# Seam work between the q phases and attention moved among GpSimd, VectorE and ScalarE in a gated cross-attention and LoRA-expert block

## The chip, the cores and the metric

One core of a Trainium2 chip runs the kernel. The metric is the device time of one execution in microseconds (us), as the median of three runs. The engines are TensorE (PE; its weight loads are shown as PEld), VectorE (DVE), ScalarE (ACT), GpSimd (POOL) and SyncE (SP), which here only issues the DMAs.

## What is computed

x is 8 batches of 128 rows of 512, all in float32. First a layer norm, then cross-attention with an RMS norm inside, 32 heads of 128, a position bias and a mask; then a second layer norm and a feed-forward layer with 28 LoRA experts, of which each row takes two.

```python
def attention(h, ctx, mask, bias, ln_w, w_q, w_k, w_v, w_out):      # h = layernorm(x)
    n = h * rsqrt(mean(h * h) + 1e-5) * ln_w
    q, k, v = n @ w_q.T, ctx @ w_k.T, ctx @ w_v.T                   # 32 heads of 128
    s = where(mask, q @ k.T + bias, -inf)
    return h + (where(mask, softmax(s), 0) @ v) @ w_out.T

x = x + tanh(g_xattn) * attention(layernorm(x), ctx, mask, ...)
x = x + tanh(g_ffn) * lora_experts(layernorm(x))
```

## The kernel before, in words

**Precision.** Every large product is made from float32 values that are split in two: a leading part ("hi", made by ScalarE with a copy that rounds) and a rest ("lo" = raw - hi, a subtraction on VectorE or GpSimd). TensorE makes three matmuls for each pair: hi hi, lo hi, hi lo. In the code `lead...` makes the first and `rest...` the second.

**Stages.** The 32 heads are worked off in 16 phases of two heads. The start makes k, v and q of phase 0 in the plain way (`q_or_k`, `v_one`) and normalises x in between: VectorE's `norm_x` makes the eight normalised tiles (`layer`, L781, and L792 with `xn_done`), TensorE turns them (`turn_xn`), ScalarE and VectorE split them (`lead_xt`, `rest_xt`), and ScalarE also keeps a raw copy (`raw_xt`).

Then q of the phases 1 to 15 is made at once in `q_phase(0)` to `q_phase(14)` with Strassen's scheme in Winograd's form: seven products of half size in place of eight. It needs four sums of x's quarters, T1 to T4 (`t_form` on VectorE at L820, `lead_t` on ScalarE, `rest_t` on VectorE; T4's rest is on GpSimd at L397), made once, and for each phase four sums of the weights, S1 to S4 (`s_forms` on GpSimd at L381 to L386, `lead_s` on ScalarE, `rest_s` on GpSimd at L391), and the parts of three plain weight blocks (`lead_a`, `rest_a` at L830). TensorE makes the products in the order A11 B11, S1 T1, A12 B21, A22 T4, S2 T2, S4 B22, S3 T3 (`product`, L1285). ScalarE copies three results, VectorE adds five (`post`, L852), the last of them from two tiles in SBUF, and SyncE stores q in DRAM and loads the next weights (`load_forms`, once the weights in w_raw[WQ] have been used).

The seam follows: GpSimd splits the weights of phase 1 (`rest(WK, 1)`, `rest(WV, 1)`, `rest(WO, 0)`), makes the additive mask from the uint8 mask (L414), adds it to the bias for two heads (`add_mask(0)`, L358), and splits w_raw[WQ], which by then holds weights of the last layer (L420). Then 15 iterations run in which TensorE makes scores of phase a, k and v of phase a + 1, P V of phase a and the output product. VectorE does bias, maximum and normalisation (`add_bias` L887 and L890, `normalise` L896 to L901) and turns the probabilities with 32x32 transposes (`turn_probs`, L909), which P V (`pv`, L1171) needs. The last layer (L1427 on) closes the kernel.

**What sets the order.** Each engine has one hand-written program that it works off strictly in order, with waits on semaphores; there is no planner. `wait_ge` holds an engine and all that is queued behind it. The names that matter: `xn_done` counts normalised tiles, `s_step` GpSimd's weight sums, `qs_hi` and `qs_lo` the parts of S, `qa_hi` and `qa_lo` those of A, `t_done`, `t_hi_done`, `t_lo_dve` and `t_lo_pool` the stages of T, `q_prod` the products, `q_copied` and `q_post` the results taken away, `comb_done` the combined bias, `w_lo_done` the rests of the weights.

Of the kernel before, what the change touches and what calls it, by code (L numbers as in the profile page):

```python
# [24 lines left out]
P = 128  # L25
# [33 lines left out]
def build(nc, x, ctx_t, weights, bias, mask, g_x, g_f, ln_w, out):  # L59
    ctx = ExitStack()  # L60
    with ctx:
# [6 lines left out]
        def bank(name):  # L68
# [10 lines left out]
        tf_hi, tf_lo = sb("tf_hi", [P, TF, 2, HALF], F32R), sb("tf_lo", [P, TF, 2, HALF], F32R)  # L79
# [38 lines left out]
        hgt_hi, hgt_lo = (t[0:ERH, 2, 0, :].rearrange("p (i e s) -> p i e s", i=2, e=2) for t in (tf_hi, tf_lo))  # L118
# [3 lines left out]
                 xt_raw[:, 2:4, HALF:], xt_raw[:, 2:4, 0:HALF]]  # L122

# [59 lines left out]
        t_hi_done, t_lo_dve, t_lo_pool = sem("t_hi_done"), sem("t_lo_dve"), sem("t_lo_pool")  # L183
# [150 lines left out]
        def _(pool):  # L334
# [14 lines left out]
            def add_mask(p):  # L349
                pool.wait_ge(bias_in, (p + 1) * 16)  # L350
                for j in range(HP):
                    if isinstance(p, int) and p == 0:

                        pool.wait_ge(t_lo_dve, 3)
# [38 lines left out]

            s_forms(0)
            rest_s(0, 0, 0)
            pool.wait_ge(t_hi_done, 2)
            pool.tensor_tensor(tf_lo[:, 3, :, :], t_raw[3], tf_hi[:, 3, :, :].bitcast(F32), ALU.subtract).then_inc(t_lo_pool, 1)  # L397
# [30 lines left out]

            add_mask(LAST)
# [9 lines left out]
        def _(act):  # L439
# [122 lines left out]
            def q_phase(i):  # L562
# [27 lines left out]
                if last:  # L590
                    return
# [121 lines left out]
        def _(dve):  # L713
# [128 lines left out]
            rest_a(0, 2, 1, 1)  # L842
            t_form(2, b_block(1, 1), b_block(0, 1))
# [10 lines left out]
            def q_phase(i):  # L854
# [5 lines left out]
                dve.wait_ge(t_lo_dve, 3) if isinstance(i, int) and i == 0 else dve.wait_ge(q_post, i * POSTS)  # L860
# [12 lines left out]
            dve.wait_ge(mask_in, 16)  # L873
            ordered(dve.tensor_reduce(row_any[:, :], mask_u8[:, :, :], AX.X, ALU.max))
# [229 lines left out]
        def _(pe):  # L1104
# [174 lines left out]
            T1, T2, T3, T4 = (tuple(f[:, n, :, :] for f in (tf_hi, tf_lo)) for n in range(TF))  # L1279
# [9 lines left out]
            def q_phase(i):  # L1289
# [6 lines left out]
                if first:  # L1296
                    pe.wait_ge(t_lo_dve, 1)
# [10 lines left out]
                if first:  # L1308
                    pe.wait_ge(t_lo_pool, 1)
# [5 lines left out]
                if first:  # L1315
                    pe.wait_ge(t_lo_dve, 2)
# [10 lines left out]
                if first:  # L1327
                    pe.wait_ge(t_lo_dve, 3)
# [238 lines left out]
```

## Time and profile before

| | |
|---|---|
| median of 3 runs | 888.44 us (887.14 to 889.11) |
| the profiled execution, its own time | 888.88 us |
| its span, first to last instruction | 887.1 us |
| busy: TensorE, weight loads | 867.6 us (98%), 768.2 us (87%) |
| busy: VectorE, ScalarE, GpSimd | 655.4 us (74%), 359.6 us (41%), 308.5 us (35%) |
| start, until the first product of the q phases | to 48 us |
| q phases | 48 to 195 us |
| attention, phases 0 to 15 | 195 to 829 us |

Times in the timelines are microseconds from the start of the span. A row of a timeline gives the start, the length, the engine, the line of the code, the operation with output and inputs, how many were merged, and in square brackets how long the engine stood idle before it and who ended that. Neighbouring operations of one engine overlap by some 0.1 us, since one is taken in while the other drains. An operation that had to wait for a port shows that as a longer duration, not as idle time. Matmuls are pipelined, so the distance between two starts says more than a duration.

### The profile page before, as it was taken

To read this page: it belongs to the slowest core of one execution; us is meant where nothing else is said; L and a number is where in the kernel's file an instruction comes from. 1 tells how busy PE (TensorE), PEld (TensorE's weight loads), DVE (VectorE), ACT (ScalarE), POOL (GpSimd) and SP (SyncE) were. 2 spreads that over 40 slices of the span, in tenths; PEclk is the share of its full clock that TensorE was granted. 3 is DMA by queue.
4 is the path that set the end of the run, shared out by engine and by line. 5 is a ranking of instruction groups with operands and counts; after the bars stand their busy time and mean duration, and the time that the engine had idled before them with its cause. 6 is when DMAs were issued, how large, how long until landed. Compare 5 with 4: busy or idle time off the path is not lost.

```text
span 887.1 us, 15278 instructions
## 1 busy us (share of the span) xinstructions
PE 867.6 (98%) x5128; PEld 768.2 (87%) x5128; DVE 655.4 (74%) x1295; ACT 359.6 (41%) x966; POOL 308.5 (35%) x218
## 2 busy tenths in 40 slices
PE   8989999998999999999999999999999999999998
PEld 7868888887998989898999989898989999898786
DVE  6885655659696877778696968778686969698863
ACT  5564444444253353434252443434252524444320
POOL 1476656686132332423142323323231423222200
PEclk9999999999999999999999999999999999999999
DMA  9124454454121221212121211203121202211001
GB/s 317 39 95 154 152 190 154 156 175 143 48 100 48 76 87 37 100 34 91 47 85 39 100 60 64 95 30 100 47 77 47 100 26 98 93 52 55 18 25 71
DMA packets 29074, 78.23 MB, mean 88 GB/s; under 512 B 4352, under 2 KB 6400, under 8 KB 27136
## 3 DMA queue, kind: packets, MB, share of 16 engines
q1 hardware_dynamic: 29056, 78.00, 25.6%
q8 instruction: 10, 0.16, 0.1%
q14 instruction: 8, 0.07, 0.0%
HBM read 60.16 MB, written 17.83 MB: 88 GB/s over the span
## 4 chain that ended last, share of the span: by engine, by line
PE 85%; DVE 8%; POOL 2%; issue 2%; DMA 1%; ACT 1%; SPq 0%; POOLq 0%; DVEq 0%; ACTq 0%
PE proj_ps L1112 53%; PE proj_ps L1285 13%; PE score_ps L1143 3%; PE score_ps L1171 3%; PE proj_ps L1463 2%; DVE attn L909 2%; PE pv_ps L1171 2%; PE turn_ps L1171 2%; PE proj_ps L1229 1%; PE pv_ps L1143 1%; PE turn_ps L1143 1%; PE proj_ps L1481 1%; DMA w_raw<-in_weights 1%; PE pv_ps L1112 1%; PE turn_ps L1112 1%
## 5 line engine op out<-in xcount | busy, mean ns | idle before, releaser
L347 POOL TENSOR_TENSOR w_lo<-w_raw,w_hi 128x1024 fp32r<-128x1024 f32 x49 | 118.4, 2417 | 360.9 <-ACT w_hi L444 287.0
L909 DVE STREAM_TRANSPOSE attn<-attn 32x256 f32<-32x256 f32 x480 | 209.1, 436 | 6.7
L1112 PE MATMUL proj_ps<-w_hi,ct_hi 128*128 128x256 f32 x512 | 146.2, 285 | 0.0
L1112 PE MATMUL proj_ps<-w_lo,ct_hi 128*128 128x256 f32 x512 | 144.8, 283 | 0.0
L1112 PE MATMUL proj_ps<-w_hi,ct_lo 128*128 128x256 f32 x512 | 144.8, 283 | 0.0
L925 DVE TENSOR_TENSOR acc<-proj_ps,acc 128x512 f32<-128x512 f32 x112 | 77.5, 692 | 66.7 <-PE proj_ps L1112 65.8
L464 ACT ACTIVATE attn<-attn,neg_max 128x128 f32<-128x128 f32 x256 | 99.2, 389 | 36.4 <-DVE neg_max L890 36.4
L444 ACT ACTIVATE w_hi<-w_raw 128x1024 fp32r<-128x1024 f32 x49 | 51.9, 1058 | 122.7 <-PE proj_ps L1112 118.8
L1112 PEld LDWEIGHTS proj_ps<-w_hi,ct_lo 128*128 128x128 f32 x512 | 98.2, 192 | 0.7
L1112 PEld LDWEIGHTS proj_ps<-w_hi,ct_hi 128*128 128x128 f32 x512 | 98.2, 192 | 0.7
L1112 PEld LDWEIGHTS proj_ps<-w_lo,ct_hi 128*128 128x128 f32 x512 | 98.1, 192 | 0.0
L358 POOL TENSOR_TENSOR comb<-mask_add,bias_sb 128x1024 f32<-128x1024 f32 x32 | 76.1, 2400 | 60.4 <-DVE attn L887 60.3
L1112 PE MATMUL proj_ps<-w_hi,tf_hi 128*128 128x512 f32 x240 | 95.2, 397 | 0.0
L1112 PE MATMUL proj_ps<-ct_hi,w_hi 128*128 128x512 f32 x240 | 94.7, 394 | 0.0
L1112 PE MATMUL proj_ps<-w_lo,tf_hi 128*128 128x512 f32 x240 | 93.7, 390 | 0.0
L1112 PE MATMUL proj_ps<-ct_hi,w_lo 128*128 128x512 f32 x240 | 93.5, 389 | 0.0
L1112 PE MATMUL proj_ps<-ct_lo,w_hi 128*128 128x512 f32 x240 | 93.4, 389 | 0.0
L1112 PE MATMUL proj_ps<-w_hi,tf_lo 128*128 128x512 f32 x240 | 93.4, 389 | 0.0
L830 DVE TENSOR_TENSOR w_lo<-w_raw,w_hi 128x256 fp32r<-128x256 f32 x45 | 36.1, 803 | 30.6 <-ACT w_hi L530 30.3
L449 ACT ACTIVATE kt<-proj_ps 128x512 f32<-128x512 f32 x64 | 37.4, 588 | 50.6 <-PE proj_ps L1112 46.6
L391 POOL TENSOR_TENSOR w_lo<-w_raw,w_hi 128x256 fp32r<-128x256 f32 x60 | 46.5, 779 | 25.3 <-ACT w_hi L535 24.9
L921 DVE TENSOR_TENSOR tf_lo<-score_ps,tf_hi 128x512 fp32r<-128x512 f32 x28 | 19.4, 692 | 46.9 <-ACT tf_hi L470 46.9
(199 smaller groups left out, 1777.6 us busy)
## 6 DMA issues: line engine op xcount, KB each, us to landing
w_raw<-in_weights SPq DMA_DIRECT2D x67, 512.0 KB, 3.3
q_spill<-attn SPq DMA_DIRECT2D x60, 256.0 KB, 3.0
qt<-q_spill SPq DMA_DIRECT2D x15, 1024.0 KB, 7.3
acc<-in_x SPq DMA_DIRECT2D x4, 512.0 KB, 8.9
bias_sb<-in_bias SPq DMA_DIRECT2D x16, 128.0 KB, 2.0
out<-attn SPq DMA_DIRECT2D x8, 256.0 KB, 2.0
w_raw<-in_x SPq DMA_DIRECT2D x6, 256.0 KB, 2.9
qt<-in_ctx_t SPq DMA_DIRECT2D x4, 256.0 KB, 5.4
```

The costliest lines, as they stand in the source:

```text
L347: pool.tensor_tensor(lo, w_raw[:, k, :], hi.bitcast(F32), ALU.subtract).then_inc(w_lo_done[k], 1)
L358: pool.tensor_tensor(comb[:, j, :, :], mask_add[:, :, :], bias_sb[:, j:j + 1, :].to_broadcast([P, B, S]), ALU.add).then_inc(comb_done, 1)
L391: pool.tensor_tensor(columns(w_lo, WO, n), columns(w_raw, WO, n), columns(w_hi, WO, n).bitcast(F32), ALU.subtract).then_inc(qs_lo, 1)
L444: act.activation(w_hi[:, k, :] if hi is None else hi, w_raw[:, k, :], ACT.Copy).then_inc(w_hi_done[k], 1)
L449: act.activation(dst, proj_ps[i][:, :], ACT.Copy).then_inc(proj_copied, 1)
L464: e = act.activation(probs[:, u, i, :], probs[:, u, i, :], ACT.Exp, bias=neg_max[:, u, i:i + 1], accum_out=row_sum[:, u, i:i + 1])
L909: tr = dve.transpose(probs_t[k:k + Q32, t, :, :, q:q + Q32].rearrange("k j b q -> k (j b) q"), probs[q:q + Q32, HP * t:HP * t + HP, :, k:k ...
L925: dve.tensor_tensor(acc[:, b, :], proj_ps[b % BANKS][:, :], acc[:, b, :], ALU.add).then_inc(acc_done, 1)
L1112: mm = pe.matmul(o, lhs(l, n), rhs(r, n), start=(start and n == 0 and m == 0), stop=(stop and n == terms - 1 and m == 2))
L1143: mm = pe.matmul(score_bank(a, u)[:, i * S:(i + 1) * S], qt[:, j, b * S:(b + 1) * S], kt[:, j, b * S:(b + 1) * S], start=True, stop=True)
L1171: mm = pe.matmul(pv_bank(a, u)[:, i * S:(i + 1) * S], v_sb[:, b, j * DH:(j + 1) * DH], probs_t[:, t, j, i, :], start=True, stop=True)
L1285: mm = pe.matmul(o[:, :], w[l][:, c, :], x[r][:, c, :], start=(start and c == 0 and m == 0), stop=(c == 1 and m == 2), skip_group_check=no ...
```

## The change

- T3 and T4, and their rests, no longer have room of their own. They lie in the parts of w_hi and w_lo that belong to WV and WK (`t_form_at`), so the buffers tf_hi and tf_lo are half as large. Hence ScalarE takes the leading parts of phase 1's K weights after product 4 of the last q phase, and those of V after product 7. Before, K's came ahead of that q phase.
- GpSimd waits for `xn_done` 8 before the first weight sums.
- T4's rest is made by VectorE, between the rests for A22 and the sum T3. One semaphore, `t_lo_done`, counts all four.
- The additive mask is made by VectorE after q phase 0, beside the reduction of the mask that was there.
- At the seam GpSimd makes the two combined biases first, then the rests of K, V and the output weights. The rest of w_raw[WQ] comes after the loop over the phases, ahead of `add_mask(LAST)`.

```diff
-        tf_hi, tf_lo = sb("tf_hi", [P, TF, 2, HALF], F32R), sb("tf_lo", [P, TF, 2, HALF], F32R)
+        tf_hi, tf_lo = sb("tf_hi", [P, 2, 2, HALF], F32R), sb("tf_lo", [P, 2, 2, HALF], F32R)
...
+        def t_form_at(s, n):
+
+            if n < 2:
+                return (tf_hi, tf_lo)[s][:, n, :, :]
+            return (w_hi, w_lo)[s][:, (WV, WK)[n - 2], :].rearrange("p (c s) -> p c s", c=2)
...
+            pool.wait_ge(xn_done, B)
             s_forms(0)
             rest_s(0, 0, 0)
-            pool.wait_ge(t_hi_done, 2)
-            pool.tensor_tensor(tf_lo[:, 3, :, :], t_raw[3], tf_hi[:, 3, :, :].bitcast(F32), ALU.subtract).then_inc(t_lo_pool, 1)
             rest_s(0, 1, 1)
...
-            rest(WK, 1)
-            pool.wait_ge(mask_in, 16)
-            pool.tensor_scalar(mask_add[:, :, :], mask_u8[:, :, :], 1.0, -NEG, ALU.subtract, ALU.mult).then_inc(mask_done, 1)
             pool.wait_ge(mask_done, 1)
             add_mask(0)
+            rest(WK, 1)
             rest(WV, 1)
             rest(WO, 0)
-            pool.wait_ge(w_hi_done[WQ], 2)
-            pool.tensor_tensor(w_lo[:, WQ, :], w_raw[:, WQ, :], w_hi[:, WQ, :].bitcast(F32), ALU.subtract).then_inc(w_lo_done[WQ], 1)
             with pool.Fori(1, LAST) as p:
...
+            pool.wait_ge(w_hi_done[WQ], 2)
+            pool.tensor_tensor(w_lo[:, WQ, :], w_raw[:, WQ, :], w_hi[:, WQ, :].bitcast(F32), ALU.subtract).then_inc(w_lo_done[WQ], 1)
             add_mask(LAST)
...
                 if first:
-                    act.wait_ge(t_lo_pool, 1)
+                    act.wait_ge(t_lo_done, 2)
...
                 if last:
+                    product(i, 4)
+                    lead(WK, 1)
+                    product(i, 7)
+                    lead(WV, 1)
                     return
...
-            lead(WK, 1)
             q_phase(NQ - 1)
-            lead(WV, 1)
-            product(NQ - 1, 7)
             lead(WO, 0)
...
             rest_a(0, 2, 1, 1)
+            rest_t(3, 2)
             t_form(2, b_block(1, 1), b_block(0, 1))
...
             dve.wait_ge(mask_in, 16)
+            dve.tensor_scalar(mask_add[:, :, :], mask_u8[:, :, :], 1.0, -NEG, ALU.subtract, ALU.mult).then_inc(mask_done, 1)
             ordered(dve.tensor_reduce(row_any[:, :], mask_u8[:, :, :], AX.X, ALU.max))
```

TensorE's waits on `t_lo_dve` and `t_lo_pool` become waits on `t_lo_done` (1, 2, 3 and 4 in the order of its products); its program is the same otherwise.

## Rows read from the trace of the kernel before

**Rows 1.** page, part 1: busy us, share of the span, instructions.

```profile
PE 867.6 (98%) x5128; PEld 768.2 (87%) x5128; DVE 655.4 (74%) x1295; ACT 359.6 (41%) x966; POOL 308.5 (35%) x218
```

**Rows 2.** Chain that ended last, in order of time: start, us, what.

```profile
60.25 113.18 PE proj_ps L1285 x498
```

**Rows 3.** Timeline of TensorE, start and first q phase (columns as told above).

```profile
41.31 0.47 PE L1112 MATMUL proj_ps<-xt_hi,w_hi 128*128 128x512 f32 x1 [0.43 <-DVE xt_lo L757]
...
56.02 0.47 PE L1285 MATMUL proj_ps<-tf_hi,w_hi 128*128 128x512 f32 x1 [1.26 <-issue]
...
60.25 0.47 PE L1285 MATMUL proj_ps<-tf_hi,w_hi 128*128 128x512 f32 x1 [1.23 <-DVE attn L852]
```

**Rows 4.** Timeline of TensorE: seam, and the same place one block later.

```profile
216.20 2.07 PE L1171 MATMUL turn_ps<-attn,v_sb 128*128 128x128 f32 x8 [3.69 <-DVE attn L909]
...
219.63 0.36 PE L1112 MATMUL proj_ps<-w_hi,ct_hi 128*128 128x256 f32 x1
...
258.40 1.06 PE L1171 MATMUL turn_ps<-attn,v_sb 128*128 128x128 f32 x8
...
260.11 0.36 PE L1112 MATMUL proj_ps<-w_hi,ct_hi 128*128 128x256 f32 x1
```

**Rows 5.** Stretches: length, busy us (instructions) of each engine, PEclk, DMA share, GB/s.

```profile
54.00:60.00 6.00, 3.75 (x16) 2.46 (x14) 5.00 (x6) 3.29 (x7) 4.82 (x5) 1.00 0.27 103
...
216.00:218.00 2.00, 1.80 (x8) 1.80 (x9) 1.83 (x7) 0.00 (x0) 0.00 (x0) 0.56 0.00 0
```

**Rows 6.** Timeline of VectorE at the seam.

```profile
196.54 2.65 DVE L852 TENSOR_TENSOR attn<-attn 128x512 f32<-128x512 f32 x1
...
203.27 0.57 DVE L898 TENSOR_TENSOR row_scale<-row_scale,row_any 128x4 f32<-128x4 f32 x1
...
203.87 2.85 DVE L901 TENSOR_TENSOR attn<-attn,row_scale 128x512 f32<-128x512 f32 x1
...
207.05 0.69 DVE L901 TENSOR_TENSOR attn<-attn,row_scale 128x512 f32<-128x512 f32 x1
```

**Rows 7.** Timeline of GpSimd at the seam.

```profile
190.21 3.64 POOL L414 TENSOR_SCALAR mask_add<-mask_u 128x1024 f32<-128x1024 uint8 x1
...
193.93 4.71 POOL L358 TENSOR_TENSOR comb<-mask_add,bias_sb 128x1024 f32<-128x1024 f32 x2
...
198.59 5.22 POOL L347 TENSOR_TENSOR w_lo<-w_raw,w_hi 128x1024 fp32r<-128x1024 f32 x2
...
203.77 2.40 POOL L420 TENSOR_TENSOR w_lo<-w_raw,w_hi 128x1024 fp32r<-128x1024 f32 x1
```

**Rows 8.** Timeline of VectorE, the sums of x and what follows.

```profile
43.50 1.23 DVE L820 TENSOR_TENSOR comb<-attn 128x1024 f32<-128x1024 f32 x1 [2.34 <-ACT attn L475]
...
49.09 3.46 DVE L830 TENSOR_TENSOR w_lo<-w_raw,w_hi 128x256 fp32r<-128x256 f32 x2
...
54.16 1.76 DVE L825 TENSOR_TENSOR tf_lo<-comb,tf_hi 128x1024 fp32r<-128x1024 f32 x1
...
60.02 0.41 DVE L830 TENSOR_TENSOR w_lo<-w_raw,w_hi 128x256 fp32r<-128x256 f32 x1
...
63.84 1.21 DVE L874 TENSOR_REDUCE row_any<-mask_u 128x8 f32<-128x1024 uint8 x1
```

**Rows 9.** Timeline of VectorE, normalisation: a pair alone, the last pair.

```profile
27.17 1.41 DVE L792 SCALAR_TENSOR_TENSOR comb<-acc,root,lnw 128x512 f32<-128x512 f32 x2
...
36.40 2.36 DVE L792 SCALAR_TENSOR_TENSOR comb<-acc,root,lnw 128x512 f32<-128x512 f32 x2
```

**Rows 10.** Timeline of GpSimd: T4's rest.

```profile
48.84 2.57 POOL L397 TENSOR_TENSOR tf_lo<-attn,tf_hi 128x1024 fp32r<-128x1024 f32 x1 [3.51 <-ACT tf_hi L540]
```

**Rows 11.** Chain that ended last: the load of the second set.

```profile
52.58 3.13 DMA w_raw<-in_weights
```

**Rows 12.** Timeline of ScalarE at the seam.

```profile
195.21 1.06 ACT L444 ACTIVATE w_hi<-w_raw 128x1024 fp32r<-128x1024 f32 x1 [3.89 <-PE proj_ps L1285]
```

**Rows 13.** Timeline of TensorE: a PV of the last blocks.

```profile
786.34 1.06 PE L1171 MATMUL turn_ps<-attn,v_sb 128*128 128x128 f32 x8
```

More of the change, by code:

```diff
@@ L117, in build @@
         at_hi, at_lo = (t[:, 0:2, :, :].rearrange("p a b s -> p (a b s)").rearrange("p (j t) -> p j t", j=HP) for t in (tf_hi, tf_lo))
-        hgt_hi, hgt_lo = (t[0:ERH, 2, 0, :].rearrange("p (i e s) -> p i e s", i=2, e=2) for t in (tf_hi, tf_lo))
+        hgt_hi, hgt_lo = (t[0:ERH, 1, 0, :].rearrange("p (i e s) -> p i e s", i=2, e=2) for t in (tf_hi, tf_lo))
         comb_flat = comb[:, :, :, :].rearrange("p h b s -> p (h b s)")
@@ L182, in build @@
         xt_raw_done, t_done = sem("xt_raw_done"), sem("t_done")
-        t_hi_done, t_lo_dve, t_lo_pool = sem("t_hi_done"), sem("t_lo_dve"), sem("t_lo_pool")
+        t_hi_done, t_lo_done = sem("t_hi_done"), sem("t_lo_done")
         s_step, qa_hi, qs_hi, qa_lo, qs_lo = sem("s_step"), sem("qa_hi"), sem("qs_hi"), sem("qa_lo"), sem("qs_lo")
@@ L352, in add_mask @@
                     if isinstance(p, int) and p == 0:
-                        pool.wait_ge(t_lo_dve, 3)
+                        pool.wait_ge(t_lo_done, TF)
                     else:
@@ L539, in lead_t @@
                 act.wait_ge(t_done, (1, 2, 4, 3)[n])
-                act.activation(tf_hi[:, n, :, :], t_raw[n], ACT.Copy).then_inc(t_hi_done, 1)
+                act.activation(t_form_at(0, n), t_raw[n], ACT.Copy).then_inc(t_hi_done, 1)
             lead_s(0, 0)
@@ L824, in rest_t @@
                 dve.wait_ge(t_hi_done, place)
-                dve.tensor_tensor(tf_lo[:, n, :, :], t_raw[n], tf_hi[:, n, :, :].bitcast(F32), ALU.subtract).then_inc(t_lo_dve, 1)
+                dve.tensor_tensor(t_form_at(1, n), t_raw[n], t_form_at(0, n).bitcast(F32), ALU.subtract).then_inc(t_lo_done, 1)
             def rest_a(i, n, j, k):
@@ L859, in q_phase @@
                 dve.wait_ge(q_copied, i * COPIES + 1)
-                dve.wait_ge(t_lo_dve, 3) if isinstance(i, int) and i == 0 else dve.wait_ge(q_post, i * POSTS)
+                dve.wait_ge(t_lo_done, TF) if isinstance(i, int) and i == 0 else dve.wait_ge(q_post, i * POSTS)
                 post(i, 5, t_sum, p6_ps[:, :], s_copy)
@@ L1278, in _ @@
             B11, B21, B22 = (tuple(x[:, 2 * k:2 * k + 2, half(t)] for x in xt2) for k, t in ((0, 0), (1, 0), (1, 1)))
-            T1, T2, T3, T4 = (tuple(f[:, n, :, :] for f in (tf_hi, tf_lo)) for n in range(TF))
+            T1, T2, T3, T4 = (tuple(t_form_at(s, n) for s in range(2)) for n in range(TF))
             def product(o, w, x, start):
@@ L1296, in q_phase @@
                 if first:
-                    pe.wait_ge(t_lo_dve, 1)
+                    pe.wait_ge(t_lo_done, 1)
                     pe.wait_ge(proj_copied, UNITS + 7)
@@ L1308, in q_phase @@
                 if first:
-                    pe.wait_ge(t_lo_pool, 1)
+                    pe.wait_ge(t_lo_done, 2)
                 else:
@@ L1315, in q_phase @@
                 if first:
-                    pe.wait_ge(t_lo_dve, 2)
+                    pe.wait_ge(t_lo_done, 3)
                     pe.wait_ge(proj_copied, PROJ0)
@@ L1327, in q_phase @@
                 if first:
-                    pe.wait_ge(t_lo_dve, 3)
+                    pe.wait_ge(t_lo_done, TF)
                 pe.wait_ge(q_post, i * POSTS + 1)
```

## The prediction

> **What bounds the kernel now.** I read the busy line of the page first: TensorE works for 98% of the span [rows 1], so nothing off it can bring more than its idle stretches, the low granted clock that may follow one, and some late issue. The chain that ended last says the same: from 60.25 us it is one run of 498 products' matmuls in 113.18 us, 0.227 us each [rows 2]; the reader is to see that no other engine has a share there. Six such matmuls make one product of the q phases: 1.36 us. So I looked, third, at TensorE's own timeline for rows with idle in front of them. They stand in two places.
>
> The start: idle before 41.31, 56.02 and 60.25 us, 0.43, 1.26 and 1.23 us [rows 3]. All three wait for VectorE or for what it feeds.
>
> The seam between the q phases and attention: 3.69 us before 216.20, waiting for VectorE's transposes [rows 4]. The clock row adds something: in 216 to 218 us the granted clock is 0.56, nearly all of it at the lower of the two levels (1.2 GHz), while after idle of 1.26 us at 56.02 it stays 1.00 [rows 5]. The price of the slow stretch: from the first PV matmul to the next projection is 219.63 - 216.20 = 3.43 us here and 260.11 - 258.40 = 1.71 us in the next block [rows 4]. So the seam holds 3.69 + 1.72 = 5.4 us, and the three places of the start 2.9 us, with some more where VectorE delays the turning of x.
>
> Then, fourth, the timelines of VectorE and GpSimd side by side. VectorE's operations with both inputs in SBUF grow when GpSimd works: the multiply of the probabilities at 203.87 takes 2.85 us, where the next one, at 207.05, takes 0.69, and ends 0.55 after GpSimd's operation of 203.77 (2.40 us) [rows 6, 7]. Those with an input in PSUM don't. Where both queues are full the rows alternate: a GpSimd piece of 256 columns holds VectorE for 0.53 us (1.76 at 54.16 against 1.23 at 43.50 for the same size; 0.6 with the handing over) [rows 8], GpSimd's of 1024 columns for up to 2.4 us.
>
> **The change part by part: the start.**
> First, GpSimd's four weight sums of set 0 wait for the eighth normalised x. Before, they ran beside it: the last two scale steps took 2.36 us, an undisturbed pair 1.41 [rows 9]. That is 0.95 us for one pair of four such; with the one-input steps between them I take 1.9 us off the normalisation. Bounds: 0 and 4 x 0.95 = 3.8. TensorE gets the last turned x earlier; then its own order (turns, six matmuls, a copy by ScalarE) binds, so the matmul of 41.31 comes 1.5 us earlier, at 39.8, and the raw copy of x, which has ScalarE's steps between, 1.2 us earlier. VectorE's activation sums begin at 42.3 instead of 43.50 [rows 8]. Queued behind GpSimd's wait are the sums and all its later pieces. They end near 40.1; ScalarE takes the first only after the raw copies, near 42.1, so the wait costs nothing. If that cover went, each us late would be one on the chain below.
>
> Second, the rest of T4 goes from GpSimd (2.57 us at 48.84) [rows 10] to VectorE (1.1 us, by the 1.23 at 43.50 less the overlap). VectorE had stood behind it: two small rests took 3.46 us at 49.09, one alone 0.41 [rows 8]. So of the stretch up to the rest of T2, which ended at 55.92 (54.16 + 1.76), 2.3 us of blocking go, 1.1 of work come, and 0.45 of waiting for ScalarE's form of A22, which was hidden. The three GpSimd rests still take a turn each, now one at T4's sum. New end: 55.92 - 1.2 - 2.3 + 1.1 + 0.45 = 53.97, and product 5 starts at 54.05 instead of 56.02.
>
> Third, the load of the next weights is issued when the rest of A22 is done: at 49.5 instead of 52.58, and by the old 3.13 us to landing it is there at about 52.65 [rows 11]. GpSimd's sums of set 1 therefore start at 52.9 and not behind VectorE's queue, but among it. VectorE after 53.97: a turn of GpSimd 0.6, rest of T3 1.1, turn 0.6, rest 0.3, turn 0.6, rest 0.3, then the first post from PSUM 0.65: 58.1. Product 7 starts at 58.2 instead of 60.25: the start brings 2.05 us. That is the term I am least sure of: with no turns lost it would be product 5's end plus product 6, 56.8 or 3.45 us gained; with every product as late as before, 0.
>
> Fourth, the mask goes to VectorE after q phase 0. The trace has no such operation there. Its price lies between 1.21 us (the reduction of the same uint8 tile, 63.84) [rows 8] and 3.64 us (the same operation on GpSimd, 190.21) [rows 7]; I take 1.2, since it is the same engine and source. Behind it are queued the small rests for phase 2, due 10 us later, and the first post of phase 1, due about 4 us after the mask's end; even 3.64 fits to within 0.3 us. Cost 0, at most 0.3.
>
> **The seam.** GpSimd's queue there was: rest of K, mask 3.64, two combined biases to 193.93 + 4.71 = 198.64, rests of V and of the output weights to 203.81, rest of WQ from 203.77 [rows 7]. VectorE's last post, of two SBUF inputs, stood from 196.54 behind the second bias and ended 199.19 [rows 6]; the multiply at 203.87 stood behind WQ. Now: biases right away (187.2 to 192.0), the rest of K after product 4 (192.3 to 194.7), which is before the q products end (195.2), so K's matmuls don't wait; the rest of V after product 7: ScalarE's form ends 195.21 + 1.06 = 196.27 [rows 12], so GpSimd holds 196.34 to 198.74, and VectorE's last post is blocked as before, to 199.3 (+0.1). The output weights go to 201.6; then GpSimd is idle. WQ has moved behind the loop. Thus at 203.3 nothing blocks: 0.40 of the small multiply (0.57 at 203.27, done as GpSimd's piece before 203.77 is) and 2.16 (2.85 against 0.69) go [rows 6]. VectorE is 2.56 - 0.1 = 2.46 us earlier, PV starts at 213.74, and TensorE's idle is 3.69 - 2.46 = 1.23. That is the length after which the clock stayed 1.00 at 56.02, so the 1.72 us of slow clock go too: the seam brings 4.2 us. Bounds: 0 if VectorE loses 2.4 us more, 5.4 if the last post isn't blocked at all.
>
> The bias piece moved up to 187 may hold a post of the phase before by 2.4 us; its reader (the copy of product 2) has 1.7 us more than it needs. WQ's rest, 2.4 us beside the last blocks, falls among VectorE's multiplies near 772 us; TensorE's PV at 786.34 has no idle before it [rows 13], and VectorE is some 3 us ahead. Cost 0, at most 2.4 if that lead is gone. The loads: nothing is issued later at the seam; the reload of x for the end waits for WQ's rest, far ahead of its reader.
>
> The Trainium skill, page "SBUF — State Buffer", section "SBUF: two separate sides", says that the pair of ports VectorE and GpSimd share is an exclusive lock, that whichever starts first has it for the whole instruction, and names no turns. Read so, a GpSimd queue that is full could keep the lock through several pieces, which speaks against feeding GpSimd earlier; the rows of this trace alternate instead, and I go by them. That reading is the no-change rival below.
>
> **Sum.** The profiled execution spans 887.1 us and took 888.88 with what lies around it; from 60 us to the seam and after it TensorE is full, so both gains reach the end. 2.05 + 4.2 = 6.2: span 880.9, execution 882.7. The median shown is 0.44 below that execution: 882.3.
>
> **Rivals.**
> (a) VectorE gets through more often. If the last post slips in before GpSimd's V piece, the remaining 1.23 goes; with half the lost turns of the start (0.7 to 1.4) saved: 880 to 881, down to 879. Against: GpSimd is ready 0.2 us before it.
> (b) One of the two gains stays out: a slow clock all the same after 1.23 us of idle (884.0), no gain at the start (884.3), or half of either: 884 to 886.5. For the clock: only one idle of that length is shown with it.
> (c) No change: the lock keeps GpSimd's queued pieces. The last post then waits for V and the output weights, 2.4 us more, which eats the 2.46 and keeps the slow clock; at the start four sums and a rest (5 x 0.7) precede the rest of T2 and product 7 comes at 60.5: 888.7. Against: the alternating rows.
> (d) Slower: the same lock, but VectorE also loses the turns of all eight GpSimd pieces of set 1 before its first post, 5.6 us instead of the 1.9 counted: 3.7 more, less the 2.05, with the seam's gain gone: 890.1. It decides from more than three further lost turns at the start with nothing left at the seam. Against: four of those pieces wait for ScalarE.
>
> **How the numbers follow.** Forecast 0.50 (881.0 to 884.0), (a) 0.17, (b) 0.17, (c) 0.09, (d) 0.07. The range 879.0 to 886.3 leaves out (c), (d) and the ends of (a) and (b). About 0.2%, 1.8 us, is what can be told from no change here: faster 0.84, same 0.09, slower 0.07.
>
> **What would show it.** In the profile after: scale steps of x undisturbed and TensorE at 39.8; product 5 near 54, product 7 near 58.2; VectorE's rest of T2 ending near 54; the last post still about 2.6 us; the multiply after it 0.69; PV about 2.5 us sooner after the last product than now and a granted clock of 1.00 there. It would be wrong if the clock falls after short idle, if ScalarE and not VectorE delays product 5, or if VectorE waits for more than one GpSimd piece at a time.

## The result, and the profile after

The changed kernel takes 882.94 us (median of 6 runs, 881.80 to 883.72) beside 888.73 us for the kernel before (6 runs): a ratio of 0.9941, with a 95% interval of 0.9925 to 0.9956. The forecast was 882.3 us, range 879.0 to 886.3. The profiled execution took 882.61 us with a span of 880.8 us. One of the eleven executions of e1_start_only below took 1072.56 us at a mean granted clock of 0.753 and is left out of its ratio.

The page's busy line stands against [rows 1]: TensorE has 2.4 us less of busy time, most of it the slow clock that went (1.6 us, below); GpSimd has 5.9 less: the mask (3.64) and the rest of T4 (2.57) went, and the two combined biases take 5.20 us at the seam where they took 4.71.

```profile
PE 865.2 (98%) x5128; PEld 765.4 (87%) x5128; DVE 653.7 (74%) x1297; ACT 359.7 (41%) x966; POOL 302.6 (34%) x216
```

TensorE's timeline, the same places as [rows 3], [rows 4] and [rows 13] and, last, the PV after that. What was line 1285 is now 1291, and 1171 is 1177.

```profile
39.17 0.47 PE L1118 MATMUL proj_ps<-xt_hi,w_hi 128*128 128x512 f32 x1 [0.28 <-DVE xt_lo L761]
...
53.35 0.47 PE L1291 MATMUL proj_ps<-tf_hi,w_hi 128*128 128x512 f32 x1 [0.83 <-issue]
...
57.43 0.47 PE L1291 MATMUL proj_ps<-w_hi 128*128 128x512 f32 x1 [1.09 <-DVE attn L857]
...
210.89 1.16 PE L1177 MATMUL turn_ps<-attn,v_sb 128*128 128x128 f32 x8 [1.20 <-DVE attn L915]
...
212.70 0.36 PE L1118 MATMUL proj_ps<-w_hi,ct_hi 128*128 128x256 f32 x1
...
779.39 1.06 PE L1177 MATMUL turn_ps<-attn,v_sb 128*128 128x128 f32 x8
791.66 1.16 PE L1177 MATMUL turn_ps<-attn,v_sb 128*128 128x128 f32 x8 [1.68 <-DVE attn L915]
```

The counterpart of the last row in the kernel before:

```profile
797.87 1.16 PE L1171 MATMUL turn_ps<-attn,v_sb 128*128 128x128 f32 x8 [0.95 <-DVE attn L909]
```

Stretches of the seam after (columns as in [rows 5]): the granted clock is 1.00 through the idle and behind it, where before it was 0.56.

```profile
209.00:211.00 2.00, 0.80 (x7) 0.60 (x7) 1.91 (x6) 0.00 (x0) 0.00 (x0) 1.00 0.23 66
211.00:213.00 2.00, 2.00 (x18) 2.00 (x19) 1.84 (x6) 0.62 (x2) 0.00 (x0) 1.00 0.00 0
```

**How to compare two traces here.** TensorE's first matmul of x with idle in front of it, for q of phase 0, stands at 31.94 us before and at 31.32 after, and in the traces below anywhere from 30.82 to 33.57, also for kernels whose program is the same up to there. What moves it lies in front of it; I call it the start-up's share. Two parts of it show in the traces. One is the wait for the first loads: the first product made from the context starts between 5.82 and 7.50 us. The other is TensorE's pace behind that. In the kernel before the granted clock is 0.50 from about 8.0 to 11.4 us, at the lower level. In e2, e3, e8, e9, e11 and e12 the first 6 to 14 matmuls stand 0.42 to 0.43 us apart too, where 0.23 is the pace of the others, though the clock row reads 1.00 there; that this is the lower level as well I infer from the pace alone. In the changed kernel and in e1 there is no such stretch. e2 has the longest (14 matmuls, each 0.2 us late: 2.8 us) and the latest first matmul of x, 33.57; e1, without one, stands at 30.94. The kernel before (TensorE, then its stretch), and e2 (the same):

```profile
7.16 0.47 PE L1229 MATMUL proj_ps<-ct_hi,w_hi 128*128 128x512 f32 x1 [1.91 <-DVE ct_lo L738]
...
8.70 0.63 PE L1229 MATMUL proj_ps<-ct_lo,w_hi 128*128 128x512 f32 x1
```

```profile
8.00:10.00 2.00, 2.00 (x7) 1.54 (x6) 1.64 (x3) 1.16 (x3) 0.00 (x0) 0.50 0.97 328
```

```profile
8.07 0.63 PE L1229 MATMUL proj_ps<-ct_hi,w_lo 128*128 128x512 f32 x1
```

```profile
8.00:10.00 2.00, 2.00 (x6) 1.54 (x5) 1.32 (x2) 1.07 (x2) 0.00 (x0) 1.00 0.96 253
```

So I read distances on TensorE's timeline, not times from the span's start. "A" is that matmul, "B" the matmul [rows 3] shows at 41.31, "7" the first matmul of product 7, "PV" the first PV of the seam, "tail" the distance between the first and second PV of phase 14 (779.39 and 791.66 above).

| kernel | A | A to B | B to 7 | 7 to PV | idle before PV | tail | span less A |
|---|---|---|---|---|---|---|---|
| before | 31.94 | 9.37 | 18.94 | 155.95 | 3.69 | 11.53 | 855.16 |
| changed | 31.32 | 7.85 | 18.26 | 153.46 | 1.20 | 12.27 | 849.48 |
| e1_start_only | 30.94 | 7.82 | 18.26 | 155.96 | 3.70 | 11.53 | 853.56 |
| e2_seam_only | 33.57 | 9.37 | 18.94 | 153.44 | 1.20 | 12.26 | 851.73 |
| e3_no_x_wait | 31.55 | 8.89 | 18.10 | 153.46 | 1.20 | 12.28 | 850.45 |
| e5_t4_on_gpsimd | 30.82 | 7.83 | 19.10 | 153.46 | 1.20 | 12.27 | 850.38 |
| e4_wq_at_seam | 31.81 | 7.83 | 18.25 | 153.89 | 1.62 | 11.53 | 849.19 |
| e7_mask_on_gpsimd | 31.02 | 7.82 | 18.28 | 153.01 | 0.76 | 12.27 | 849.08 |
| e12_mask_and_wq | 31.50 | 7.82 | 18.26 | 155.16 | 2.94 | 11.53 | 850.40 |
| e6_mask_and_half_wq | 32.02 | 7.84 | 18.27 | 154.09 | 1.83 | 11.53 | 849.48 |
| e8_wq_after_bias | 32.48 | 7.82 | 18.25 | 153.47 | 1.21 | 11.53 | 848.72 |
| e9_v_after_post | 32.35 | 7.83 | 18.28 | 152.06 | 0 | 12.28 | 848.05 |
| e10_start_order | 31.96 | 7.85 | 17.00 | 153.52 | 1.21 | 12.27 | 848.24 |
| e11_all_three | 32.35 | 7.83 | 16.98 | 152.15 | 0 | 11.53 | 846.05 |

The span's 6.3 us are then: 0.62 in front of A, the start-up's, which is not the change's; 1.52 from A to B; 0.68 from B to 7; 2.49 from 7 to PV; 1.62 from PV to the next projection (3.43 before, 212.70 - 210.89 = 1.81 after); and 0.63 lost behind it, of which 0.74 in the tail. Without the start-up the change is worth 855.16 - 849.48 = 5.68 us, and the medians differ by 5.79.

### The profile page after: what moved, and what is told of

It is laid out like the page before. It is cut to its first block, busy times and chain, and to the rows that moved or that the text cites. A ratio compares the mean times of both kernels' runs of the same rounds, so it can differ in the third digit from the quotient of the medians.

```text
span 880.8 us, 15280 instructions
## 1 busy us (share of the span) xinstructions
PE 865.2 (98%) x5128; PEld 765.4 (87%) x5128; DVE 653.7 (74%) x1297; ACT 359.7 (41%) x966; POOL 302.6 (34%) x216
## 4 chain that ended last, share of the span: by engine, by line
PE 86%; DVE 8%; issue 1%; DMA 1%; ACT 1%; POOL 1%; SPq 1%; DVEq 0%; POOLq 0%
PE proj_ps L1118 53%; PE proj_ps L1291 15%; PE score_ps L1149 3%; PE score_ps L1177 3%; PE proj_ps L1469 2%; DVE attn L915 2%; PE pv_ps L1177 2%; PE turn_ps L1177 2%; PE pv_ps L1149 1%; PE turn_ps L1149 1%; PE proj_ps L1487 1%; DMA acc<-in_x 1%; PE pv_ps L1118 1%; PE turn_ps L1118 1%; DVE attn L893 1%
## 5 line engine op out<-in xcount | busy, mean ns | idle before, releaser
L834 DVE TENSOR_TENSOR w_lo<-w_raw,w_hi 128x256 fp32r<-128x256 f32 x45 | 33.1, 737 | 29.3 <-ACT w_hi L533 29.1
L1118 PEld LDWEIGHTS proj_ps<-w_lo,tf_hi 128*128 128x128 f32 x240 | 45.0, 188 | 9.7
```

The lines of the kernel that those rows point to most:

```text
L1118: mm = pe.matmul(o, lhs(l, n), rhs(r, n), start=(start and n == 0 and m == 0), stop=(stop and n == terms - 1 and m == 2))
```

## The experiments

Each runs beside the kernel before on its own chip; a ratio is to that one (888.68, 888.12 or 888.84 us). The table above holds their distances. Where a diff leaves a part out, the rest is as in the changed kernel.

### Does each half bring what its own steps say?

**e1_start_only** is the changed kernel with the seam as before: mask, rests and WQ on GpSimd in the old order, ScalarE's leading parts in the old places, and with them T3 and T4 in room of their own (only GpSimd's part of the diff is shown).

```diff
+            rest(WK, 1)
+            pool.wait_ge(mask_in, 16)
+            pool.tensor_scalar(mask_add[:, :, :], mask_u8[:, :, :], 1.0, -NEG, ALU.subtract, ALU.mult).then_inc(mask_done, 1)
             pool.wait_ge(mask_done, 1)
             add_mask(0)
-            rest(WK, 1)
             rest(WV, 1)
             rest(WO, 0)
+            pool.wait_ge(w_hi_done[WQ], 2)
+            pool.tensor_tensor(w_lo[:, WQ, :], w_raw[:, WQ, :], w_hi[:, WQ, :].bitcast(F32), ALU.subtract).then_inc(w_lo_done[WQ], 1)
             with pool.Fori(1, LAST) as p:
```

> The kernel before with the edits of the start alone: GpSimd's first weight sums wait for the eighth normalised x, and VectorE makes T4's rest. Mask, seam and the rest of WQ stay as they were. Theory (the two engines block each other whole instructions at a time): the last pair of scale steps takes 1.41 us and not 2.36, product 7 of phase 0 starts 2.0 to 2.9 us earlier than at 60.25, the seam is unchanged (3.7 us idle before the first PV, granted clock near 0.56 behind it); 886.6 us, 2.1 below before. Rival (the 2.8 us by which the changed kernel's product 7 is earlier come from loads that happened to land earlier): within 0.5 us of before, 888.5.

**e2_seam_only** is the kernel before with only the seam part of the change, T3 and T4 in room of their own too. So no run tests the shared room by itself.

> The kernel before with the edits of the seam alone: mask on VectorE, the two biases first, K's and V's leading parts after products 4 and 7, WQ's rest behind the loop; the start is untouched. Theory: the multiply of the probabilities takes 0.69 us and not 2.85, 1.2 us idle before the first PV, granted clock 1.00 there, and 0.7 us more idle before the second PV of phase 14, where WQ's rest now blocks VectorE: -2.5 - 1.6 + 0.7 = -3.4, 885.3 us. Rival (the seam's gain needs the earlier start, or the clock falls all the same): 887 to 888.

Measured: e1 887.07 us, ratio 0.9981 (0.9972 to 0.9990); e2 885.29 us, ratio 0.9960 (0.9947 to 0.9974). In the table e1 has the changed start and the old seam to 0.04 us, and e2 the reverse: the halves don't touch each other. The gains in the medians, 1.6 and 3.4 us, add to 5.0 of the 5.8.

Why is e1's share 1.6 and not 2.2, in "span less A" too? Its TensorE idled 3.70 us like the kernel before, but in the profiled execution its slow stretch is longer. Timelines of TensorE and VectorE and stretches, e1:

```profile
212.98 2.08 PE L1177 MATMUL turn_ps<-attn,v_sb 128*128 128x128 f32 x8 [3.70 <-DVE attn L915]
...
200.64 2.86 DVE L907 TENSOR_TENSOR attn<-attn,row_scale 128x512 f32<-128x512 f32 x1
```

```profile
210.00:212.00 2.00, 0.00 (x0) 0.00 (x0) 1.94 (x5) 0.00 (x0) 0.00 (x0) 0.80 0.20 66
212.00:214.00 2.00, 1.02 (x5) 1.02 (x5) 1.87 (x7) 0.00 (x0) 0.00 (x0) 0.50 0.00 0
214.00:216.00 2.00, 2.00 (x11) 2.00 (x11) 1.87 (x7) 0.60 (x1) 0.78 (x1) 0.50 0.00 0
216.00:218.00 2.00, 2.00 (x11) 2.00 (x11) 1.95 (x5) 1.08 (x2) 1.59 (x1) 0.50 0.02 4
218.00:220.00 2.00, 2.00 (x19) 2.00 (x18) 1.95 (x5) 0.00 (x0) 0.00 (x0) 1.00 0.60 172
```

The clock fell while TensorE was still idle and stayed at 0.50 to 218, 5.0 us of matmuls at half speed where the kernel before has 3.4: its clock fell only as the matmuls began again, at about 216.2, and was back at 219.6 ([rows 5] and the stretch behind it).

```profile
218.00:220.00 2.00, 2.00 (x13) 2.00 (x12) 1.92 (x5) 0.69 (x2) 1.56 (x1) 0.59 0.01 4
```

That is 2.5 us lost against 1.7. The price of a slow stretch isn't fixed: I had one sample of it. These are two single executions; whether the same makes the difference in the medians, no trace shows.

### What of the start is the wait for x, what is T4?

**e3_no_x_wait** takes GpSimd's wait for the eighth normalised x out again.

```diff
-            pool.wait_ge(xn_done, B)
             s_forms(0)
```

> The changed kernel without GpSimd's wait for the eighth normalised x. Theory: the scale steps are blocked again (2.36 us for the last pair), the matmul that waits for the last x comes 1.2 to 1.5 us later, and so do products 5 and 7: 884.2 us, 1.3 above the changed kernel's 882.9. Rival (moving T4's rest is all that counts at the start): no later product 7, 882.9.

**e5_t4_on_gpsimd** gives the rest of T4 back to GpSimd, between the first two pieces of the weights, with a semaphore of its own.

```diff
             rest_s(0, 0, 0)
+            pool.wait_ge(t_hi_done, 2)
+            pool.tensor_tensor(t_form_at(1, 3), t_raw[3], t_form_at(0, 3).bitcast(F32), ALU.subtract).then_inc(t_lo_pool, 1)
...
-            rest_t(3, 2)
```

> The changed kernel with T4's rest back on GpSimd, in its old place; GpSimd's wait for x stays. Theory: VectorE's rest for A12 is blocked for 2 us again, but starts from an earlier point; product 5 comes 0.4 us and product 7 0.8 us later than in the changed kernel: 883.7 us. Together with the wait's share (1.2 to 1.5 us) that makes up the 2.1 of the start. Rival (T4's rest was the whole gain of the start): product 7 comes 2 us later, 884.9.

Measured: e3 884.42 us, ratio 0.9954 (0.9939 to 0.9970); e5 883.48 us, ratio 0.9948 (0.9932 to 0.9965). In distances e3 is 1.04 worse from A to B and 0.16 better from B to 7, so the wait is worth 0.88; e5 is 0.84 worse from B to 7 (0.69 of it up to product 5, where 0.4 was expected), so T4's move is worth 0.84. Together that is 1.72 of the start's 2.20. The other 0.48 is not a part of the change. VectorE's scale steps and GpSimd's first sum, in e3:

```profile
34.00 0.75 DVE L795 SCALAR_TENSOR_TENSOR comb<-acc,root,lnw 128x512 f32<-128x512 f32 x1
...
35.54 2.35 DVE L795 SCALAR_TENSOR_TENSOR comb<-acc,root,lnw 128x512 f32<-128x512 f32 x2
```

```profile
34.53 0.80 POOL L387 TENSOR_TENSOR w_raw<-w_raw 128x256 f32<-128x256 f32 x1 [3.24 <-DMA w_raw<-in_weights]
```

and the same in the kernel before:

```profile
34.39 1.22 DVE L792 SCALAR_TENSOR_TENSOR comb<-acc,root,lnw 128x512 f32<-128x512 f32 x1
```

```profile
33.99 1.07 POOL L381 TENSOR_TENSOR w_raw<-w_raw 128x256 f32<-128x256 f32 x1 [3.15 <-DMA w_raw<-in_weights]
```

GpSimd's sums start when their load lands. There it was before the third scale step (1.22 us), in e3 after it (0.75): 0.47 us by when a load lands. e2, which has the old start too, goes with the kernel before (9.37), so e3 is one trace against two, and why its load lands later isn't shown. The medians speak for the larger figure: each against the kernel before on its own chip, e3 gains 4.3 us and the changed kernel 5.8, 1.5 more. So without the wait the collision costs between 1.04 and 1.52 us from A to B in these traces; the wait takes the collision away for good (the last pair is 1.41 after, at 34.89, where [rows 9] have 2.36) and with it this dependence.

### Which of the moved pieces at the seam counts?

The forecast put the gain of 2.46 us down to both the mask and WQ's rest leaving GpSimd's queue. Four kernels put them back: **e7_mask_on_gpsimd** the mask alone, **e4_wq_at_seam** WQ's rest alone (behind the output weights), **e12_mask_and_wq** both, **e6_mask_and_half_wq** the mask and half of WQ's rest. GpSimd's part of e12 (VectorE's mask and the later WQ rest, which go, are not shown):

```diff
+            pool.wait_ge(mask_in, 16)
+            pool.tensor_scalar(mask_add[:, :, :], mask_u8[:, :, :], 1.0, -NEG, ALU.subtract, ALU.mult).then_inc(mask_done, 1)
             pool.wait_ge(mask_done, 1)
             add_mask(0)
             rest(WK, 1)
             rest(WV, 1)
             rest(WO, 0)
+            pool.wait_ge(w_hi_done[WQ], 2)
+            pool.tensor_tensor(w_lo[:, WQ, :], w_raw[:, WQ, :], w_hi[:, WQ, :].bitcast(F32), ALU.subtract).then_inc(w_lo_done[WQ], 1)
```

> The changed kernel with the rest of WQ back at the seam, right behind the rest of the output weights; nothing else is undone, the mask stays on VectorE. Theory: GpSimd is then busy until about 201.1 us where VectorE needs its two SBUF inputs from 200.5: the small multiply or the one after it is blocked until GpSimd ends, some 0.6 us, PV comes 0.6 us later and its idle is 1.8 us; the 0.7 us at the second PV of phase 14 go: 882.8 us, no change. Rival (WQ's rest at the seam was what made PV late by 2.5 us and slowed the clock): idle 3.7 us, clock 0.56 behind it, 886.3 us.

> The changed kernel with the mask made by GpSimd again, ahead of the two biases at the seam; WQ's rest stays behind the loop. Theory: GpSimd ends its queue near 200.5 us instead of 198.7, VectorE's last post is blocked by the rest of K instead of V and ends 0.7 us earlier, the small multiply waits 0.9 us; PV comes at about the same time (idle 1.0 to 1.6 us, clock 1.00): 883.0 us, no change. Rival (the mask's 3.6 us on GpSimd are what made PV late): idle 3 us or more, 885 to 887.

> The changed kernel with both put back on GpSimd at the seam: the mask ahead of the biases and WQ's rest behind the rest of the output weights. Each of them alone was worth 0.6 us or less by this theory, since VectorE needs its two SBUF inputs at one moment only; both together keep GpSimd busy until about 203 us, the multiply of the probabilities is blocked for 2.2 us, the idle before the first PV is 3.3 to 3.5 us and the clock behind it falls: 885.8 to 886.5 us (+2.2 and 1.7, less 0.7 at the second PV of phase 14). Rival (the order biases first, then K, is what brings the gain): 883.5 us or less.

> As the kernel with both put back, but only the first half of WQ's rest (512 columns, 1.3 us) stands at the seam, the second half stays behind the loop. Theory: the multiply is blocked for about 1.0 us, the idle before the first PV is 2.2 to 2.5 us; whether the granted clock falls after idle of this length is what is asked (it stayed 1.00 after 1.2 us and fell after 3.7). If it stays: 884.0 us; if it falls: 885.6 us.

Measured: e4 882.91 us, ratio 0.9935 (0.9920 to 0.9950); e7 882.21, 0.9933 (0.9917 to 0.9950); e12 885.04, 0.9972 (0.9955 to 0.9990); e6 883.44, 0.9943 (0.9927 to 0.9960). The idle before PV is 1.20 us with neither, 0.76 with the mask, 1.62 with WQ, 1.83 with mask and half of WQ and 2.94 with both. For e6 2.2 to 2.5 was expected and for e7 1.0 to 1.6. The parts don't add: put back alone, the mask gains 0.45 us from 7 to PV and WQ costs 0.43; put back together they cost 1.70. And e12 with both back is still 0.79 us better there than the kernel before (155.16 against 155.95). What is left of the change in it is the order, the biases before the rest of K: its last addition takes 1.89 us where it took 2.65 [rows 6]. GpSimd and VectorE in e12:

```profile
195.14 5.22 POOL L353 TENSOR_TENSOR w_lo<-w_raw,w_hi 128x1024 fp32r<-128x1024 f32 x2
200.31 2.40 POOL L425 TENSOR_TENSOR w_lo<-w_raw,w_hi 128x1024 fp32r<-128x1024 f32 x1
```

```profile
199.81 0.57 DVE L905 TENSOR_TENSOR row_scale<-row_scale,row_any 128x4 f32<-128x4 f32 x1
200.42 2.85 DVE L908 TENSOR_TENSOR attn<-attn,row_scale 128x512 f32<-128x512 f32 x1
```

and in e4:

```profile
199.14 2.41 POOL L423 TENSOR_TENSOR w_lo<-w_raw,w_hi 128x1024 fp32r<-128x1024 f32 x1
```

```profile
200.99 0.58 DVE L904 TENSOR_TENSOR row_scale<-row_scale,row_any 128x4 f32<-128x4 f32 x1
201.60 0.69 DVE L907 TENSOR_TENSOR attn<-attn,row_scale 128x512 f32<-128x512 f32 x1
```

VectorE needs two inputs from SBUF at two moments only, the last addition and the multiplies; between them it reads PSUM. What counts is which GpSimd piece runs at these moments. With the mask in front, WQ's rest starts at the very moment the small multiply is done and holds the large one (2.85); without the mask it is over before (0.69). In e7 the mask is free, since the pieces behind it only move from one place where nobody asks for the port to another. The last addition even fares better, 1.89 us for 2.72, because the piece in front of it starts earlier. VectorE in e7,

```profile
193.41 1.89 DVE L859 TENSOR_TENSOR attn<-attn 128x512 f32<-128x512 f32 x1
```

then the changed kernel, VectorE and GpSimd:

```profile
193.72 2.72 DVE L857 TENSOR_TENSOR attn<-attn 128x512 f32<-128x512 f32 x1
...
200.72 0.69 DVE L907 TENSOR_TENSOR attn<-attn,row_scale 128x512 f32<-128x512 f32 x1
```

```profile
193.53 5.18 POOL L353 TENSOR_TENSOR w_lo<-w_raw,w_hi 128x1024 fp32r<-128x1024 f32 x2 [1.67 <-ACT w_hi L447]
```

**The clock.** e12 was to show 3.3 to 3.5 us of idle and a falling clock. The idle was 2.94, and in the profiled execution the clock stayed (e12, stretches):

```profile
211.00:213.00 2.00, 0.26 (x2) 0.26 (x3) 1.89 (x6) 0.00 (x0) 0.00 (x0) 1.00 0.20 59
213.00:215.00 2.00, 2.00 (x20) 2.00 (x20) 1.86 (x6) 0.77 (x2) 0.02 (x1) 1.00 0.00 0
```

Its five executions have spans of 881.9, 881.9, 883.2, 884.3 and 885.0 us at mean granted clocks of 1.000, 1.000, 0.998, 0.998 and 0.996. So after about this idle the clock sometimes falls and sometimes doesn't, which would explain the median of 885.04 over a profiled 883.74; that the three longer ones fell at the seam I infer from the means, since only one was profiled. For it speaks that the 43 executions of the ten kernels with at most 1.62 us of idle there (the changed one, e2 to e5, e7 to e11) all have a mean of 0.999 or 1.000; e6, with 1.83, has one of 0.998 in four. At the seam no trace shows the clock lower after 0.8 to 1.8 us, both do after 3.7.

The trace of the kernel before has a second fall, which I overlooked: TensorE is idle for 1.53 us at the start of the span and for 1.91 us before 7.16, and from about 8.0 us the granted clock is 0.50. So the length of one idle doesn't decide it alone, and how much room my step "idle back to 1.23, so the clock stays" had isn't known.

### The losses left over, and the version without them

The changed kernel shows three places where VectorE and GpSimd still meet on the path. In the tail (GpSimd, then VectorE; [rows 13] have no idle at the first PV, and the second had 0.95 before):

```profile
761.69 2.36 POOL L353 TENSOR_TENSOR w_lo<-w_raw,w_hi 128x1024 fp32r<-128x1024 f32 x1 [7.14 <-ACT w_hi L447]
764.00 2.40 POOL L431 TENSOR_TENSOR w_lo<-w_raw,w_hi 128x1024 fp32r<-128x1024 f32 x1
```

```profile
765.53 0.90 DVE L904 TENSOR_TENSOR row_scale<-row_scale,row_any 128x4 f32<-128x4 f32 x1
```

**e8_wq_after_bias** moves WQ's rest behind the last combined bias.

```diff
-            pool.wait_ge(w_hi_done[WQ], 2)
-            pool.tensor_tensor(w_lo[:, WQ, :], w_raw[:, WQ, :], w_hi[:, WQ, :].bitcast(F32), ALU.subtract).then_inc(w_lo_done[WQ], 1)
             add_mask(LAST)
+            pool.wait_ge(w_hi_done[WQ], 2)
+            pool.tensor_tensor(w_lo[:, WQ, :], w_raw[:, WQ, :], w_hi[:, WQ, :].bitcast(F32), ALU.subtract).then_inc(w_lo_done[WQ], 1)
```

> The changed kernel with the rest of WQ moved behind the last combined bias, so that GpSimd makes it while VectorE turns probabilities. Theory: what the changed kernel lost near 765 us is that this 2.4 us rest stands at once behind the rest of the output weights and holds VectorE's small multiply. Moved, the small multiply is back to about 0.17 us and the second P V of phase 14 has 0.95 us of idle ahead of it where it had 1.68: time 0.7 us below the changed kernel, 882.2. Rival: the 0.7 us belongs to something else in the last blocks (the reload of x): the idle stays 1.68 and the time 882.9. A second rival: the combined bias is what blocks there, and WQ's rest behind it blocks a later multiply, for the same 0.7.

**e9_v_after_post** lets the last addition go ahead of the rest of V.

```diff
             rest(WK, 1)
+            pool.wait_ge(q_post, NQ * POSTS)
             rest(WV, 1)
```

> The changed kernel with GpSimd waiting for the last result to be added before it makes the rest of V at the seam. Theory: the last addition, now 2.72 us because that rest is 0.2 us ahead of it, falls to about 0.7; the rests of V and of the output weights come 0.8 us later than they did, and the second of them may hold the small multiply by up to 0.75. Idle before the first P V 1.20 falls to 0 to 0.2, time 881.7 (1.2 less). Rival: VectorE only loses the same wait one operation later, where it meets the rest of V or of the output weights at its additions of bias: idle 1.2 still, 882.9. Slower than that if V's matmuls now wait for the rest of V: TensorE would show idle ahead of them, up to 0.8 us.

**e10_start_order** holds GpSimd's weight sums of the second set until the rests of T are made, and has ScalarE take the second part of A of set 1 before the form S1.

```diff
             rest_s(0, 3, 2)
+            pool.wait_ge(t_lo_done, TF)
...
+                    product(0, 3)
+                    lead_a(1, 1, 0, 1)
...
+                if first:
+                    lead_s(1, 0)
```

> The changed kernel with two edits at the start. GpSimd waits for the rests of all activation sums before it makes the weight sums of the second set, and ScalarE takes the second part of A of set 1 before the form S1 of set 1 (it then makes S1 after the q copy). Theory: the idle of 0.83 us before product 5 and of 1.09 us before product 7 are GpSimd's pieces between VectorE's rests of T2, T3 and the small ones. Without them product 5 starts at 52.8 (53.35 in the changed kernel) and product 7 at 55.5 to 55.8 (57.43): 1.6 to 1.9 us less, 881.0. Rival: ScalarE's forms, not GpSimd's pieces, release these products; then both stay where they are, 882.9. Other rival: GpSimd's later sums come late for set 1's products, TensorE waits 1 to 2 us near 66 us, and the gain is given back: 882.5 to 883.5.

**e11_all_three** has all of them.

> The changed kernel with all three: the rest of WQ behind the last combined bias, the rest of V behind the last addition, and the new order at the start. They lie at three places between which TensorE is full, so by theory they add: 0.7 + 1.2 + 1.9 = 3.8 us less than the changed kernel, 879.1. If the seam's wait and the end's give nothing, 881.0; if they all only shift waits, 882.9.

Measured: e8 882.79 us, ratio 0.9931 (0.9915 to 0.9948); e9 882.01, 0.9924 (0.9907 to 0.9941); e10 881.93, 0.9922 (0.9906 to 0.9939); e11 879.99, 0.9901 (0.9884 to 0.9917). By "span less A" against the changed kernel: 0.76, 1.43, 1.24 and 3.43 us; the first three add up to the fourth. e11 was put at 879.1 and is 0.9 above that, 0.7 of it because the start brought 1.2 and not 1.9. e8 was put at 882.2 and is 0.6 above, though its mechanism is there to 0.02 us; its A stands 1.16 later than that of the changed kernel: ten of its first matmuls stand 0.43 us apart, and its first product starts 0.56 later. Its median is only 0.15 below the changed kernel's of another chip, which alone would not be told from nothing; what bears it out is the tail, 11.53 against 12.27, with the multiply back at 0.16 in front of it (e8, VectorE and GpSimd):

```profile
766.66 0.16 DVE L904 TENSOR_TENSOR row_scale<-row_scale,row_any 128x4 f32<-128x4 f32 x1
```

```profile
769.30 4.75 POOL L364 TENSOR_TENSOR comb<-mask_add,bias_sb 128x1024 f32<-128x1024 f32 x2 [4.12 <-DVE attn L893]
774.02 2.39 POOL L432 TENSOR_TENSOR w_lo<-w_raw,w_hi 128x1024 fp32r<-128x1024 f32 x1
```

In e9 the wait is nearly all gone and not merely moved: the addition takes 0.68, the small multiply pays 0.6 for it, and PV has no idle (VectorE, then TensorE).

```profile
194.71 0.68 DVE L858 TENSOR_TENSOR attn<-attn 128x512 f32<-128x512 f32 x1
...
199.47 0.77 DVE L905 TENSOR_TENSOR row_scale<-row_scale,row_any 128x4 f32<-128x4 f32 x1
```

```profile
210.52 0.31 PE L1178 MATMUL turn_ps<-attn,v_sb 128*128 128x128 f32 x1
```

In e10 product 5 still waits 0.83 us, product 7 no longer does (TensorE). What holds product 5 are, by the rows, GpSimd's two pieces of set 0 from 49.31 on, which the edit doesn't move; of my 1.6 to 1.9 only the idle before product 7 was to be had.

```profile
53.99 0.47 PE L1297 MATMUL proj_ps<-tf_hi,w_hi 128*128 128x512 f32 x1 [0.83 <-issue]
```

```profile
49.31 3.50 POOL L397 TENSOR_TENSOR w_lo<-w_raw,w_hi 128x256 fp32r<-128x256 f32 x2 [3.65 <-ACT w_hi L539]
55.44 0.86 POOL L387 TENSOR_TENSOR w_raw<-w_raw 128x256 f32<-128x256 f32 x1 [2.63 <-DVE w_lo L835]
```

e11 beats both kernels: 0.8 to 1.2% below the kernel before, and 3 us below the changed one's median on another chip.

## Why the prediction was right, step by step

**Wait for x: the mechanism right, the size in part luck.** Foretold 1.5 us at B; A to B fell by 1.52. But e3 shows 1.04 as the wait's own part in its profiled execution, and 0.88 once B to 7 is counted; the rest hangs on when the load lands.

**T4 and product 5.** Foretold 54.05 and 58.2 for products 5 and 7; they came at 53.35 and 57.43, or 53.97 and 58.05 with A where it was. T4's move was worth 0.84 (e5). The turns went as the alternating rows said: from 49.80 on three long operations in a row each lose one GpSimd piece, 0.53 to 0.55 us, and none loses two (VectorE after; the row at 48.66 is one undisturbed).

```profile
48.66 1.22 DVE L829 TENSOR_TENSOR w_lo<-attn,w_hi 128x1024 fp32r<-128x1024 f32 x1
49.80 1.77 DVE L824 TENSOR_TENSOR attn<-attn 128x1024 f32<-128x1024 f32 x1
51.50 1.75 DVE L829 TENSOR_TENSOR tf_lo<-comb,tf_hi 128x1024 fp32r<-128x1024 f32 x1
53.17 1.75 DVE L829 TENSOR_TENSOR w_lo<-attn,w_hi 128x1024 fp32r<-128x1024 f32 x1
```

So rivals (c) and (d), in which a full queue keeps the port, fell. The Trainium skill, page "SBUF — State Buffer", section "SBUF: two separate sides", calls the shared port pair an exclusive lock held for the whole instruction; the trace agrees as far as one instruction goes (+0.53 us on 1.22, about one piece), and shows beyond the page that it changes hands between two.

**The mask: the price missed, the outcome right.** I bounded it by 1.21 and 3.64 us; it took 0.69, outside both.

```profile
61.02 0.69 DVE L879 TENSOR_SCALAR mask_add<-mask_u 128x1024 f32<-128x1024 uint8 x1
```

The nearest row, the reduction of the same tile, shared engine and source but not the kind of operation. In e10, where GpSimd has four pieces queued at that point, it took 1.23, so it too can be held by a GpSimd piece. (The Trainium skill, page "VectorE: DVE Perf Modes", section "The perf-mode tier table", gives float32 `tensor_scalar` in SBUF 1227 ns for 2048 elements, twice the rate of `tensor_tensor`; 0.69 us for 1024 agrees, here from a uint8 source.) It hides as forecast.

**The seam: the sum right, one of its reasons too many.** Foretold 2.46 us less idle and 1.72 of slow clock; measured 2.49 and 1.62. The last addition was blocked as said (2.72), the multiply fell to 0.69 as said. But the text put this down to WQ leaving, where e4 has WQ at the seam and still 0.69: for the large multiply either move alone was enough, and 0.79 us of the 2.49 stays with the order alone (e12). A row that is right after an edit doesn't tell which edit made it so. The slow clock went as forecast, but on thinner ground than the text says: it rests on idles of 1.26 and 1.23 us alone, and passes over the fall behind the 1.91 us at 7.16 in the same trace.

**WQ's late rest: the step that failed.** "Cost 0, at most 2.4" was 0.73 us. I looked at the PV of 786.34, which had no idle, and took VectorE to be 3 us ahead in all the last blocks. The PV behind it, at 797.87, already had 0.95 us of idle waiting for VectorE. There was no lead there, and what VectorE lost, TensorE lost. e4, with WQ at the seam, has the same median as the changed kernel (882.91): the move gained 0.43 at the seam and lost 0.74 at the end, 0.3 us in all in distances, too little to tell in the medians.

**The total.** 2.05 + 4.2 foretold, 2.20 + 4.11 measured, less 0.63 behind the seam: 5.68 us for 6.2. In the execution that was profiled the span came out at 880.8 for 880.9, and that is luck: 0.62 us in front of A, the start-up's, hide the 0.63 lost behind the seam. The median of 882.94 lies 0.6 above the forecast, about the size of the term that was taken as 0.

## What to carry to other kernels

When two engines share a port, don't count how much work one of them has, but list the moments at which the other needs the port on the critical path, and see which piece runs then; a piece is free everywhere else, and moving it can cost nothing, everything or, with another one, more than the sum. Put each side piece where the partner does work that doesn't take the port (here its transposes, of which 16 took 7.18 us beside a GpSimd bias and 7.17 alone, or its reads of PSUM, 0.68 us beside GpSimd's rests). Before calling a moved piece covered, look at every place behind it where the bounding engine already idles on the engine that pays, not at the nearest one.

## What the runs showed of the hardware that I had not expected

- The subtract-and-multiply of a uint8 tile of 128x1024 into float32 takes 0.69 us on VectorE and 3.64 on GpSimd, where GpSimd's two-input subtraction of the same size in float32 takes 2.40: on GpSimd the one-input operation is the dearer one.
- TensorE's granted clock stayed 1.00 through an idle of 2.94 us in one execution, and fell with idles of 3.69 and 3.70, once as the matmuls began again and once 1.8 us before. It also fell in the kernel before at about 8.0 us, behind an idle of only 1.91. Once down it cost 1.7 us in one execution (3.4 us at the lower level) and 2.5 in another (5.0 us of matmuls at 0.50), after the same idle.
- What lies before the first matmuls of x moves everything behind it by up to 2.75 us from trace to trace (A at 30.82 to 33.57), which is more than most of what was studied here. It holds the first loads and, in 7 of the 14 traces, 6 to 14 of the first matmuls at half pace, which the clock row shows in one of them only. Distances taken behind it, where the programs are the same, repeat to within 0.1 us.
